# Expert stage of a four-layer kernel on one core: a quarter of the low one-hots moved from VectorE to GpSimd, the gathers reordered, and the weighing split around a tile's first choice

## The reference

```python
q = (xn @ w_q.T).reshape(b, s, 2, NH, KD).transpose(2, 0, 1, 3, 4)      # NH = 8 heads
sim = jnp.einsum('pbnhd,hkpd->pbnhk', q, keys_p)                         # 2 x 32 keys a head
scores, idx = jax.lax.top_k(sim, K)                                      # K = 8: the first choice
all_scores = scores[0][..., :, None] + scores[1][..., None, :]
all_idx = idx[0][..., :, None] * NK + idx[1][..., None, :]
sc, pk = jax.lax.top_k(all_scores, K)                                    # the second choice
indices = jnp.take_along_axis(all_idx, pk, axis=-1)                      # 64 experts a token, of 1024
hmid = jnp.einsum('bnd,bnhkd->bnhk', inputs, down[indices])
hmid = jax.nn.sigmoid(sc) * jax.nn.gelu(hmid, approximate=False)
return jnp.einsum('bnhk,bnhkd->bnd', hmid, up[indices])
```

## Time and profile before

| | |
|---|---|
| median of 3 runs | 542.76 us (540.2 to 550.87) |
| profiled execution | 542.56 us |
| its span, first to last instruction | 540.8 us |
| mean granted TensorE clock | 0.766 of 2.4 GHz |
| busy: DVE, PE, ACT, POOL | 86%, 72%, 56%, 34% |
| last layer | from about 290 us to the end |

### The profile page before, as it was taken

One profiled execution on the slowest core, in us unless ns is written; L12 is line 12 of the kernel. 1 busy time (PEld: TensorE's weight loads), 2 busy tenths in 40 slices (PEclk: granted clock), 3 DMA queues, 4 the chain that ended last, 5 costly groups with the idle time before them and its releaser, 6 DMA issues. The chain is left out here.

```text
span 540.8 us, 16061 instructions
## 1 busy us (share of the span) xinstructions
PE 390.4 (72%) x6356; PEld 271.0 (50%) x6356; DVE 467.1 (86%) x2059; ACT 300.4 (56%) x625; POOL 184.5 (34%) x209
## 2 busy tenths in 40 slices
PE   2997579877798769776345846767887878785575
PEld 1662466555555555456342325555564545545575
DVE  5387998899978998997954999999999999999992
ACT  1433455186434754238421678483968787778551
POOL 3454229632683129423511540304040403040001
PEclk9999895999688996977555885757576765858577
DMA  4800000000000000000000000000000000000000
GB/s 93 235 34 0 1 1 2 2 1 1 1 2 1 1 1 2 1 1 1 2 1 0 1 1 4 4 14 2 4 13 2 13 3 14 2 13 2 13 3 21
DMA packets 12473, 6.95 MB, mean 13 GB/s; under 512 B 3182, under 2 KB 11758, under 8 KB 12398
## 3 DMA queue, kind: packets, MB, share of 16 engines
q1 hardware_dynamic: 11366, 5.65, 3.8%
q10 hardware_dynamic: 1032, 0.27, 0.2%
HBM read 4.87 MB, written 1.05 MB: 11 GB/s over the span
## 5 line engine op out<-in xcount | busy, mean ns | idle before, releaser
L1820 ACT ACTIVATE hot_last<-iota_f,lo_last 128x128 f16<-128x128 f32 x240 | 72.8, 393 | 0.3 <-DVE lo_last L1946 0.3
L2137 PE MATMUL psum<-hot_w,hot_lo 64*128 64x8 f16 x2688 | 39.7, 164 | 39.8 <-DVE hot_lo L1970 26.0
L2137 PEld LDWEIGHTS psum<-hot_w,hot_lo 64*128 64x128 f16 x2688 | 37.8, 101 | 56.4 <-DVE hot_lo L1970 29.9
L1970 DVE TENSOR_TENSOR hot_lo<-lo_t,iota_lo 128x4096 f16<-128x4096 f16 x24 | 53.5, 2285 | 0.0
L2084 PE MATMUL psum<-x3t,down_t 128*128 128x512 f32 x64 | 45.9, 842 | 1.7 <-PEq L319 1.7
L1730 POOL TENSOR_TENSOR eq<-eq,side_f 128x1024 f16<-128x1024 f16 x14 | 29.0, 2088 | 48.9 <-DVE eq L1924 48.9
L1893 DVE FIND_INDEX8 side_i<-side,keysims 128x8 uint32<-128x32 f32 x256 | 41.6, 192 | 0.0
L1300 PE MATMUL psum<-we,x1t 128*128 128x512 f32 x64 | 39.6, 731 | 2.3 <-DVE wexp L875 1.1
L1738 POOL TENSOR_TENSOR rstd<-rstd,minus_half 128x2 f32<-128x2 f32 x8 | 5.7, 707 | 104.3 <-DVE rstd L2025 104.3
L1386 PE MATMUL psum<-q_hi,k_t 32*128 32x128 f16 x256 | 21.2, 264 | 19.1 <-DVE masked L952 13.1
L679 POOL TENSOR_TENSOR s_lo<-feat,s_hi 128x512 f16<-128x512 f32 x28 | 31.7, 1159 | 8.6 <-ACT s_hi L487 8.6
(11 more groups left out here) (281 smaller groups left out, 1113.2 us busy)
## 6 DMA issues: line engine op xcount, KB each, us to landing
xall<-in_L_attn_x SPq DMA_DIRECT2D x4, 256.0 KB, 4.6
out<-o SPq DMA_DIRECT2D x8, 128.0 KB, 1.8
we<-in_L_ffn_We SPq DMA_DIRECT2D x1, 512.0 KB, 4.3
downn<-in_L_ffn_down SPq DMA_DIRECT2D x1, 512.0 KB, 5.3
upw<-in_L_ffn_up SPq DMA_DIRECT2D x1, 512.0 KB, 6.3
wh<-in_L_attn_W_h SPq DMA_DIRECT2D x1, 256.0 KB, 3.2
keysn<-in_L_ffn_keys_p SPq DMA_DIRECT2D x1, 256.0 KB, 5.5
wqkv<-in_L_attn_w_qkv ACTq DMA_DIRECT2D x1, 192.0 KB
```

What stands on the lines that cost most here:

```text
L1820: ins = nc.scalar.activation(hot_last[:, lane], iota_f[:], ACT.Abs, bias=lo_last[:, lane:lane + 1], scale=-1.0)
L1970: nc.vector.tensor_tensor(hot_lo[:, pairs], bc(lo_t[:, lanes].rearrange("p (j s) -> p j s", s=2).unsqueeze(2), [P, LB // 2, P, 2]), bc(v.i ...
L2137: ins = nc.tensor.matmul(bank[2 + q // 2 * 2 + t][:, c:c + EH], low, hot_w[half, i, lane // 2, :, lane % 2], start=(lane % (2 * LB) == 0 a ...
```

## The change

GpSimd makes the third quarter (q = 2) of the low one-hots of every pair, one operation a lane, 32 in all (`mid_one_hots`), ahead of its other work for the pair. It starts when `lo_last_ok` is there and when both of VectorE's remaining L1970 operations are done (`hot_ok` counts two a pair now). VectorE has two L1970 operations a pair instead of three. `lo_last` has 64 columns instead of 32. TensorE gathers in the order 0, 1, 3, 2; `key_scores(2p+4)` stays in front of the last gather, `key_scores(2p+5)` behind it. VectorE's `weigh(p)` is split: first half, first choice of tile 2p+4, second half, first choice of tile 2p+5. In the last pair the four mixes follow the gather order. One semaphore (`upw_ok`) is merged into another.

```diff
-        hot_ok, g_mm, mix_ok = sem("hot_ok", QB - 1), sem("g_mm", QB), sem("mix_ok", QB)
+        hot_ok, g_mm, mix_ok = sem("hot_ok", QB - 2), sem("g_mm", QB), sem("mix_ok", QB)
...
+    GATHER_ORDER = (0, 1, 3, 2)
...
+                def mid_one_hots(p):
+                    pool.wait_ge(lo_last_ok.h, p + 1)
+                    wait(pool, hot_ok, p)
+                    for lane in range(LB):
+                        ins = nc.gpsimd.tensor_scalar(hot_mid[:, lane], iota_f[:], lo_last[:, lane:lane + 1], None,
+                                                      ALU.is_equal)
+                    ins.then_inc(hot_mid_ok.h, 1)
...
                 for p in range(-1, PAIRS):
+                    if p >= 0:
+                        mid_one_hots(p)
                     if p >= 1:
                         root(p - 1)
...
-                    last = slice(LB * (QB - 1), LB * QB)
+                    last = slice(LB * (QB - 2), LB * QB)
...
-                    for q in range(QB - 1):
+                    for q in range(QB - 2):
...
                     if p >= 0:
-                        weigh(p)
+                        weigh(p, (0,))
                     if p + 2 < PAIRS:
-                        for u in (2 * p + 4, 2 * p + 5):
-                            first_choice(u)
+                        first_choice(2 * p + 4)
+                    if 0 <= p < PAIRS - 1:
+                        weigh(p, (1,))
+                    if p + 2 < PAIRS:
+                        first_choice(2 * p + 5)
...
-                    if q < QB - 1:
+                    if q < QB - 2:
                         wait(pe, hot_ok, p, q + 1)
+                    elif q == QB - 2:
+                        pe.wait_ge(hot_mid_ok.h, p + 1)
...
-                    for q in range(QB - 1):
-                        for c in early[q:q + 1]:
+                    for i, q in enumerate(GATHER_ORDER[0:QB - 1]):
+                        for c in early[i:i + 1]:
                             hidden(p // PB + 1, c)
                         gathered(p, q)
                     if p + 2 < PAIRS:
                         key_scores(2 * p + 4)
-                    gathered(p, QB - 1)
+                    gathered(p, GATHER_ORDER[QB - 1])
                     if p + 2 < PAIRS:
                         key_scores(2 * p + 5)
```

More of the change, by code:

```diff
@@ L1668, in peer @@
         w_t, w_hi, w_lo = sb("w_t", [P, P]), sb("w_hi", [P, P], F16), sb("w_lo", [P, P], F16)
-        lo_t, hi_t = sb("lo_t", [P, P - LB], F16), sb("hi_t", [P, P], F16)
-        hot_lo = sb("hot_lo", [P, (P - LB) // 2, P, 2], F16)
-        lo_last, iota_f, hot_last = sb("lo_last", [P, LB]), sb("iota_f", [P, P]), sb("hot_last", [P, LB, P], F16)
+        lo_t, hi_t = sb("lo_t", [P, P - 2 * LB], F16), sb("hi_t", [P, P], F16)
+        hot_lo = sb("hot_lo", [P, (P - 2 * LB) // 2, P, 2], F16)
+        lo_last, iota_f, hot_last = sb("lo_last", [P, 2 * LB]), sb("iota_f", [P, P]), sb("hot_last", [P, LB, P], F16)
+        hot_mid = sb("hot_mid", [P, LB, P], F16)
         hot_hi = sb("hot_hi", [P, P // 2, EH, 2], F16)
@@ L1694, in peer @@
         o4_ok, stored = sem("o4_ok"), (sem("stored0", 16), sem("stored1", 16))
-        upw_ok = sem("upw_ok")
+        hot_mid_ok = sem("hot_mid_ok")
         own = sem("dve_own4", 0)
@@ L1751, in _ @@
                 arrived(pool, "peer")
-                nc.gpsimd.tensor_scalar(v.upw[:], v.upw[:], 1.0 / WEIGHT_SCALE, None, ALU.mult).then_inc(upw_ok.h, 1)
+                nc.gpsimd.tensor_scalar(v.upw[:], v.upw[:], 1.0 / WEIGHT_SCALE, None, ALU.mult).then_inc(zeroed.h, 1)
                 nc.gpsimd.memset(hot_wide[:], 0.0).then_inc(zeroed.h, 1)
                 for p in range(-1, PAIRS):
+                    if p >= 0:
+                        mid_one_hots(p)
                     if p >= 1:
@@ L1819, in last_one_hots @@
                     for lane in range(ACT_LANES(p)):
-                        ins = nc.scalar.activation(hot_last[:, lane], iota_f[:], ACT.Abs, bias=lo_last[:, lane:lane + 1],
+                        ins = nc.scalar.activation(hot_last[:, lane], iota_f[:], ACT.Abs, bias=lo_last[:, LB + lane:LB + lane + 1],
                                                    scale=-1.0)
@@ L1948, in one_hots @@
                     nc.vector.scalar_tensor_tensor(w_lo[:], w_t[:], WEIGHT_SCALE, w_hi[:], ALU.mult, ALU.subtract)
-                    nc.vector.scalar_tensor_tensor(lo_t[:], hi_t[:, 0:P - LB], -float(P), number[:, 0:P - LB], ALU.mult, ALU.add)
+                    nc.vector.scalar_tensor_tensor(lo_t[:], hi_t[:, 0:P - 2 * LB], -float(P), number[:, 0:P - 2 * LB], ALU.mult, ALU.add)
                     step(nc.vector.tensor_tensor(
@@ L1953, in one_hots @@
                     if p == PAIRS - 1:
-                        dve.wait_ge(zeroed.h, 2)
+                        dve.wait_ge(zeroed.h, 3)
                     for i, w in enumerate((w_hi, w_lo)):
@@ L1986, in last_lanes, with weigh @@
                         bc(v.iota_lo[:].unsqueeze(1), [P, LB // 4, P, 2]), ALU.is_equal).then_inc(hot_ok.h, 1)
-                def weigh(p):
+                def weigh(p, halves=(0, 1)):
                     b, at = p // PB, 2 * (p % PB)
@@ L1994, in weigh @@
                     if p == PAIRS - 1:
-                        for q in range(QB):
-                            wait(dve, g_mm, p, q + 1)
+                        for i, q in enumerate(GATHER_ORDER):
+                            wait(dve, g_mm, p, i + 1)
                             lanes = slice(LB * q, LB * q + LB)
@@ L2002, in weigh @@
                         return
-                    for half in range(2):
+                    for half in halves:
                         wait(dve, g_mm, p, 2 * half + 2)
@@ L2112, in gathered @@
                         if p == PAIRS - 1:
-                            pe.wait_ge(hot_ok.h, (QB - 1) * PAIRS + 1)
+                            pe.wait_ge(hot_ok.h, (QB - 2) * PAIRS + 1)
                     if p:
@@ L2121, in gathered @@
                                 at, c = lane - LB * q, 2 * EH * (lane - LB * q)
-                                if q < QB - 1:
+                                if q < QB - 2:
                                     low = hot_lo[:, lane // 2, :, lane % 2]
+                                elif q == QB - 2:
+                                    low = hot_mid[:, at, :]
                                 elif at < ACT_LANES(p):
@@ L2135, in gathered @@
                                 half, c = slice(HK * t, HK * t + HK), EH * (lane % (2 * LB))
-                                low = hot_lo[half, lane // 2, :, lane % 2] if q < QB - 1 else hot_last[half, lane - LB * q, :]
+                                if q < QB - 2:
+                                    low = hot_lo[half, lane // 2, :, lane % 2]
+                                else:
+                                    low = (hot_mid, hot_last)[q - (QB - 2)][half, lane - LB * q, :]
                                 ins = nc.tensor.matmul(
                                     bank[2 + q // 2 * 2 + t][:, c:c + EH], low, hot_w[half, i, lane // 2, :, lane % 2],
-                                    start=(lane % (2 * LB) == 0 and i == 0), stop=(i == 1), skip_group_check=True)
+                                    start=(lane == LB * q and q in (0, 3) and i == 0), stop=(i == 1), skip_group_check=True)
                     ins.then_inc(g_mm.h, 1)
@@ L2166, in _ @@
                 decoded(0)
-                pe.wait_ge(upw_ok.h, 1)
+                pe.wait_ge(zeroed.h, 2)
                 for p in range(PAIRS):
```

## The result

The changed kernel takes 636.24 us (median of 4 runs, 634.12 to 638.01), the kernel before 546.82 (median of 4, 540.2 to 552.05): a ratio of 1.1733, 95% interval 1.1685 to 1.1782. The ratios in this document leave out a kernel's slow executions (here the 550.87 and 552.05 of the kernel before), so they are not the quotients of the medians. The profiled execution took 634.12 us with a span of 632.4. The direction was forecast, the size was not: 28.2 us were expected on the profiled execution's 542.56, and 91.6 came, far above the range's top of 600.

What follows compares the result with a forecast made beforehand. Bound: ScalarE's quarter, gather 3 and VectorE's 9.6 us tail, 28.96 us a pair. 10.4 (pairs 2 to 5) + 1.5 + 3.7 + 6.0 + 6.6 (pairs 0, 1, 6, 7) = 28.2 on 542.56: 570.8 us; range 553 to 600.

Steps and rivals of the forecast that it cites:

- What bounds the kernel before: Pairs 2 to 5: ScalarE's quarter, gather 3 and VectorE's 9.6 us tail make the 28.96 us period.
- The key scores behind gather 3: On TensorE, key scores 2p+4 now follow gather 3: 2.6 us more for each of pairs 2 to 5, 10.4 in all.
- Rival D: VectorE alone bounds the kernel, so each of seven periods loses 2.2 + 1.0 us: 520 us; chance 0.04.
- Rival C: TensorE's clock rises, shortening key scores and ScalarE's wait: period 29.1 us, total 543.5 us; chance 0.11.
- Rival B: GpSimd costs little, the key scores alone cost: 561 us, down to 553; chance 0.16.
- GpSimd's price, d: Time from one GpSimd one-hot operation's start to the next: 0.30 us taken, ends 0.11 and 0.46.
- the 0.38: Sign of a wrong forecast: GpSimd's spacing above 0.38 us, where `normal` starts after +21.3 and ScalarE's copy waits on GpSimd.
- The end of the range, 0.46: Upper end of GpSimd's spacing per operation, 0.35 + 0.11 us: period 36.7 us, total 611 us.
- Rival A: Slow GpSimd, 0.40 to 0.46 us an operation, sets the period: 597 to 611 us; chance 0.19.
- The blocking, c: GpSimd's operations wait out VectorE's eight two-input operations of `rows_columns` and `which_side`: 2.8 us a pair.
- The chain behind the lanes: After GpSimd's lanes (+19.6): `root` 0.9, ScalarE's `normal` 0.8, copy 0.6, to +21.9; a tie in pairs 2 to 5.
- Pair 6: No key scores; `last_numbers` adds 2.4 us of blocking, GpSimd ends at +22.0: 28.5 against 22.53 us, +6.0.

Runs made afterwards that it cites:

- the split: Kernel before, with only the second half of the weighing moved between the first choices of tiles 2p+4 and 2p+5: 543.41 us, ratio 0.9935.
- The run with seven forms: Changed kernel with GpSimd's 32 operations in another form in each of pairs 1 to 6 (such as subtract, two steps, 16 elements): 613.09 us in its only execution.

## Why the prediction was wrong in size

**What bounds the kernel before.** Right. VectorE's wait for gather 3 and the 9.6 us behind it are the period: shorten the wait alone (the split) and 0.8 to 0.9 us a pair come back, as the 28.2 expected of that run said.

**The key scores behind gather 3.** Right, term by term: +2.6 a pair forecast, 31.37 to 31.56 us found when GpSimd is taken out. Rival D, VectorE as the only bound, falls with it. Rival C, a rise of TensorE's clock, did not come either: the key scores of pair 2 still take 2.07 us, and the granted clock of pairs 2 to 5 is 0.56 to 0.65 of 2.4 GHz, where it was 0.65 to 0.71 before. Rival B falls with d, below.

**GpSimd's price, d.** This is the step that failed: "I take 0.30 (0.19 + 0.11), as the pointer scalar row is the nearest in operands." It is 0.58 where nothing disturbs it and 0.61 over a pair. It lies above the 0.38 that the prediction had named as a sign of being wrong, with the consequence named there: `normal` starts at +27.6 and the copy waits on GpSimd. Two readings went wrong. The 763 ns for 512 elements were scaled down to 128 by proportion, as if there were no start cost in them; the same two-step form is 0.43 apart at 128 elements and 0.75 at 512, so it has 0.84 ns an element and a start of 0.32. And the start cost was taken from two-input sums (0.11), another kind of operation. The end of the range, 0.46, was built with the same 0.11, so it was no end. The constant product of the earlier trace rows was the row to go by, as it has a single step: a line through its 2.79 us at 1024 and 0.58 at 128 has 2.5 ns an element and a start of 0.26, just what the run with 16 elements shows. From the one size on record the split of the price could not be read. Rival A had the right row and the wrong start; its top, 611 at d = 0.46, still lies 23 us below the measured 634.

**The blocking, c.** Too large: 2.8 us forecast, 1.0 found (undisturbed, 32 lanes take 31 x 0.577 + 0.60 = 18.5 of the 19.51). "Each GpSimd operation then waits for one of these" is not what happens, and neither is VectorE's wait of up to 8 x d:

```profile
415.52 1.31 POOL L1747 TENSOR_SCALAR hot_mid<-iota_f,lo_last 128x128 f16<-128x128 f32 x1
```
```profile
414.29 0.46 DVE L1934 SCALAR_TENSOR_TENSOR ahead_of<-rc,best_i 128x128 f32<-128x128 f16 x1
415.11 1.34 DVE L1942 TENSOR_TENSOR eq<-rc,iota_r 128x1024 f16<-128x1024 f16 x2
```

In pair 2 the lane beside `which_side` takes 1.31 instead of 0.60; those beside the four short operations of `rows_columns` grow by 0.03 to 0.12. VectorE's L1934 takes 0.46 instead of 0.285, L1942 1.34 instead of 1.29 for its two. The largest growth beside a lane is L1929's in pair 0, 0.667 instead of 0.227; no VectorE operation was held up by a whole lane. The rule of the Trainium skill ("SBUF — State Buffer", Who interferes with whom: only the shared port pair causes contention, and it is an exclusive lock) agrees with one side here, the 4.50 us of a blocked lane, and not with the other, where a VectorE operation lost at most 0.44 us to lanes of 0.60. The error in c hid some of the error in d: with d = 0.58 and the prediction's c the lanes would have ended at 12.1 + 23.6 x 0.58 + 2.8 = +28.6, 2 us after the +26.55 found.

**The chain behind the lanes.** Right, and it carries the right answer once d is right: +6.9 + 19.5 = +26.4; `root`, `normal` and copy, 2.3, make +28.7; 9.6 more give 38.3 against 38.47 found. In pair 0 there is no `root`; gather 2, key scores 2p+5, their copy and one first choice follow, 26.4 + 1.87 + 2.07 + 0.6 + 4.2 = 35.1 against 35.34. Pair 7: 8.5 + 19.5 + 1.87 + 0.65 = +30.5 against +15.6 before, 14.9 longer, 15.7 found. The run with seven forms shows that the period follows GpSimd's lanes, and the run with `root` moved that it did so through `root` and `normal` rather than through the late gather.

**Pair 6.** 26.4, plus 1.8 for one lane blocked by `last_numbers` (21.30 us for the 32), 0.9, 2.5 and 3.04: 34.6 against 35.05 found. Here the forecast of 2.4 for such blocking was near.

With d and c as measured and nothing else changed, the sum is 7.9 + 10.5 + 4 x 9.4 + 12.1 + 14.9 = 83 us, where the span grew by 91.6 less the 6.35 ahead of the stage, 85.2.

## What to carry to other kernels

Price an operation moved to another engine as start plus slope, from two rows of the same form at different sizes, never from one row by proportion; in 32 operations of 0.58 us, 32 starts of 0.25 are 8 us. Before relieving the busiest engine, find the wait that ends last in the period: here a second chain ran 1 us behind the first, and putting the key scores on the wrong side of a gather cost 2.6 us a pair, more than the 2.2 that VectorE was relieved of. Ask of every operation put at the head of an in-order queue who waits for what stood there before: a `root` of 0.9 us kept a copy, and with it the whole period, waiting for 19.5 us of one-hots.

## What the runs showed of the hardware that was not expected

- A GpSimd tensor-by-scalar operation costs about 0.25 us to start; with one step it then takes 2.55 ns an element, and with two steps less in all (0.43 instead of 0.58 us for 128, undisturbed). Pointer or constant, comparison or subtraction, f32 or f16 made no difference (19.43 to 19.55 us for 32).
- Beside back-to-back two-input operations of VectorE a GpSimd operation that reads does not get a turn (4.50 us instead of 0.60), while VectorE loses 0.15 us over 6.8 us.
- TensorE's row of 128 small matmuls sometimes breaks off for 1.2 to 1.9 us with no semaphore behind it ("issue"). It is harmless while something else ends later, and on the path as soon as two gathers and a key score stand in a row. Two neighbouring pauses lie 128 matmuls with their weight loads apart, and a packet of the queue called "instruction" starts ahead of each; that late instructions are the cause is inferred, and no run shows it.
